# Routed experts of a decoder: one region of rows per expert, routing in five groups of batches, 23 pairs of tiles for 24

## The reference, cut to what matters

```python
logits = x @ gate_w.T                      # 2048 x 8
top, which = top_k(logits, 2)
weight = softmax(top)
y = sum over k of weight[k] * (silu(x @ gate[which[k]].T) * (x @ up[which[k]].T)) @ down[which[k]].T
out = layernorm(x + y)
```

## Time and profile before

| | us |
|---|---|
| median of 3 runs | 3531.8 |
| the profiled execution | 3559.3 |
| its span | 3557.3 |
| TensorE busy in the span | 3178.6 (89%) |
| VectorE busy | 2074.4 (58%) |
| GpSimd busy | 1446.6 (41%) |
| ScalarE busy | 1284.7 (36%) |

### The profile page before, as it was taken

How to read it: one execution, slowest core, us unless ns; L and a number is a source line. 1 busy time by engine, 2 the same in 40 slices (tenths; PEclk the granted TensorE clock), 3 DMA queues, 4 the chain that set the end, 5 groups by cost and what they waited for, 6 DMA issues and landing times. The chain is left out here.

```text
span 3557.3 us, 59026 instructions
## 1 busy us (share of the span) xinstructions
PE 3178.6 (89%) x21124; PEld 2638.1 (74%) x21124; DVE 2074.4 (58%) x3713; ACT 1284.7 (36%) x3287; POOL 1446.6 (41%) x1473
## 2 busy tenths in 40 slices
PE   7999999999969999799896999699999999459992
PEld 5887878878757777677685777588888888258991
DVE  4666666576636666411164666467666677235556
ACT  2333333333256666211103333244444444124440
POOL 3454344444322443300262222355555556155445
PEclk9999999999979999799998999799999999679996
DMA  4001003021120100449472111410101000166664
GB/s 166 21 17 48 0 27 123 0 65 55 52 68 28 51 26 23 182 147 342 150 166 81 39 38 36 142 36 30 34 23 36 22 12 9 43 219 227 241 222 154
DMA packets 129172, 302.42 MB, mean 85 GB/s; under 512 B 18601, under 2 KB 30633, under 8 KB 126466
## 3 DMA queue, kind: packets, MB, share of 16 engines
q1 hardware_dynamic: 111938, 263.14, 22.1%
q0 software_dynamic: 15360, 36.25, 3.8%
q10 hardware_dynamic: 1728, 1.07, 0.1%
HBM read 236.90 MB, written 77.60 MB: 88 GB/s over the span
## 5 line engine op out<-in xcount | busy, mean ns | idle before, releaser
L377 POOL TENSOR_TENSOR a_sq<-a_tq,a_sinq 128x256 f32<-128x256 f32 x128 | 150.1, 1192 | 359.1 <-DVE a_tq L448 359.1
L377 POOL TENSOR_TENSOR a_sk<-a_tk,a_sink 128x256 f32<-128x256 f32 x128 | 123.8, 987 | 90.0 <-DVE a_tk L448 90.0
L343 ACT COPY a_probT<-bank 128x512 f32<-128x512 f32 x64 | 37.5, 586 | 329.0 <-PE bank L653 329.0
L390 POOL TENSOR_TENSOR e_sk<-e_tk 128x512 f32<-128x512 f32 x64 | 66.6, 1040 | 211.2 <-DVE e_tk L475 211.2
L975 POOL TENSOR_TENSOR d_prob<-d_prob,d_nmax 128x1024 f32<-128x1024 f32 x32 | 63.9, 1998 | 197.4 <-DVE d_nmax L1072 197.4
L330 ACT ACTIVATE a_sm<-a_sm,a_nmax 128x128 f32<-128x128 f32 x256 | 99.8, 391 | 121.9 <-DVE a_nmax L535 121.9
L335 ACT ACTIVATE e_prob<-bank,e_nb,e_rq 128x128 f32<-128x128 f32 x256 | 113.8, 455 | 83.1 <-DVE e_nb L540 83.1
L881 ACT ACTIVATE b_prob<-bank,b_nb 128x128 f32<-128x128 f32 x512 | 139.0, 386 | 10.7 <-DVE b_nb L1077 10.3
L2213 POOL TENSOR_TENSOR n_wu_lo<-n_wu,n_wu_hi 128x1408 fp32r<-128x1408 f32 x24 | 77.3, 3221 | 125.0 <-DVE n_wu_hi L2254 125.0
L470 DVE TENSOR_TENSOR a_kr<-a_kr,a_sk 128x512 f32<-128x512 f32 x64 | 66.5, 1038 | 88.9 <-POOL a_sk L377 88.9
L1074 DVE TENSOR_REDUCE b_nmax<-bank 128x8 f32<-128x1024 f32 x64 | 77.7, 1214 | 64.9 <-PE bank L1213 64.5
(11 more groups left out here) (501 smaller groups left out, 10650.6 us busy)
## 6 DMA issues: line engine op xcount, KB each, us to landing
n_wg<-in_f_wg SPq DMA_DIRECT2D x24, 704.0 KB, 4.4
n_wu<-in_f_wu SPq DMA_DIRECT2D x24, 704.0 KB
cw_wg<-in_c_wg SPq DMA_DIRECT2D x32, 512.0 KB
cw_wu<-in_c_wu SPq DMA_DIRECT2D x32, 512.0 KB
cw_wd<-in_c_wd SPq DMA_DIRECT2D x32, 512.0 KB
packed<-all_zero SPq DMA_DIRECT2D x32, 384.0 KB, 4.2
n_xe<-packed SPq DMA_DIRECT2D x48, 256.0 KB
n_wd<-in_f_wd SPq DMA_DIRECT2D x24, 512.0 KB
```

Of the source, the lines that this page charges most:

```text
L343: nc.scalar.copy(probT[:], pP[:, :]).then_inc(act_pt, 1)
L377: step = nc.gpsimd.tensor_tensor(o, i, s, ALU.mult)
```

## The change

The stages `logits_only`, `route` and `dispatch` become one, `spread_routing`. The 16 batches are cut into five groups of 2, 2, 4, 4 and 4. For each batch TensorE makes four transposes and four products with the turned batch as the loaded side, and the router's 8 columns as the moving one, so that the logits come out with tokens in the partitions. VectorE selects group g, then places group g - 1 (for which TensorE has counted), and GpSimd sends a group as soon as it is placed.

For that, the row of a token must not hang on the counts of other experts: `packed2` gets a fixed region of 2048 rows for each expert (16384 rows in all, where it had 6144). After the last group VectorE works out the pairs' experts, the tile at which each pair's rows begin in its region, and the rows in the packed result, which stays as it was. SyncE waits for these tables and loads the weights of the first two pairs in this stage; the weights' buffers and semaphores move to `RoutedWeights`, a stage around both. In `routed_experts` SyncE reads a tile number beside the expert number for each pair. The number of pairs is no longer rounded up to an even one: 23 for 24, 46 tiles for 48, and `in_turns` writes a rest of two tiles out behind the last whole round. Zeroing covers the regions: 128 partitions x 4 rows x 2 KB = 1024 KB for each of the 32 transfers.

```diff
-def in_turns(engine, slot, rounds, ring):
+def in_turns(engine, slot, rounds, ring, rest=0):
     slot(0, 0, back=False)
     with engine.Fori(0, rounds - 1) as i:
@@ -1363,7 +1363,9 @@
             slot(i, n)
         slot(i + 1, 0)
     for n in range(1, ring):
-        slot(rounds - 1, n, ahead=n < ring - 1)
+        slot(rounds - 1, n, ahead=n < ring - 1 or rest > 0)
+    for n in range(rest):
+        slot(rounds, n, ahead=n < rest - 1)
...
+def spread_routing(nc, name, psum, tri, ones, ident, xall, w_dram, packed, NE, weight, rows, weights, NP):
...
+    K, PAIR = 2, 2 * P
+    GROUPS = ((0, 2), (2, 2), (4, 4), (8, 4), (12, 4))
...
+            sp.dma_start(rw[:], w_dram["rw"]).then_inc(c_in, 16)
             sp.dma_start(iota[:], w_dram["iota"]).then_inc(c_in, 16)
+            sp.wait_ge(tabled, 2)
+            for w in range(2):
+                weights.load(sp, weights.number(sp, 0, w), w)
+        def _(pool):
+            for g, (b0, size) in enumerate(GROUPS):
+                pool.wait_ge(v_p, g + 1)
+                for b in range(b0, b0 + size):
+                    for k in range(K):
+                        nc.gpsimd.indirect_dma_start(packed, bass.IndirectOffsetOnAxis(ap=target[:, b, k:k + 1], axis=0), xall[:, b, :],
+                                                     None, bounds_check=NE * REGION - 1, oob_is_err=False).then_inc(sent, 16)
+            pool.wait_ge(sent, 16 * K * B)
...
+            def select(g):
+                b0, size = GROUPS[g]
+                own = slice(b0, b0 + size)
+                dve.wait_ge(pe_l, done(b0 + size - 1))
+                vec.tensor_copy(logits[:, own].rearrange("p b e -> p (b e)"), pL[g % 2][:, 0:NE * size]).then_inc(v_l, 1)
+                dve.wait_ge(v_l, g + 1)
+                for b in range(b0, b0 + size):
+                    last = vec.max(top[:, b], logits[:, b])
                 step(last)
+                for b in range(b0, b0 + size):
+                    last = vec.max_index(topi[:, b], top[:, b], logits[:, b])
                 step(last)
+                step(vec.tensor_copy(topf[:, own], topi[:, own]))
+                each = [P, K, size, NE]
+                step(vec.tensor_tensor(hot[:, :, own], iota[:, 0:NE].unsqueeze(1).unsqueeze(1).to_broadcast(each),
+                                       topf[:, own, 0:K].rearrange("p b k -> p k b").unsqueeze(3).to_broadcast(each), ALU.is_equal))
+                vec.tensor_tensor(sel[:, own], hot[:, 0, own], hot[:, 1, own], ALU.add).then_inc(v_sel, 1)
+            def place(g):
+                b0, size = GROUPS[g]
+                own = slice(b0, b0 + size)
+                dve.wait_ge(pe_c, g + 1)
+                for n in range(size):
+                    step(vec.tensor_tensor(carry[:, b0 + n + 1], carry[:, b0 + n], pC[g % 2][:, P + NE * n:P + NE * n + NE], ALU.add))
+                step(vec.tensor_tensor(pos[:, own], pC[g % 2][:, 0:NE * size].rearrange("p (b e) -> p b e", b=size), carry[:, own], ALU.add))
+                step(vec.tensor_tensor(prod[:, :, own], hot[:, :, own], pos[:, own].unsqueeze(1).to_broadcast([P, K, size, NE]), ALU.mult))
+                step(vec.tensor_reduce(rowf[:, own].rearrange("p b k -> p k b"), prod[:, :, own], AX.X, ALU.add))
+                vec.tensor_copy(target[:, own], rowf[:, own]).then_inc(v_p, 1)
+            for g in range(len(GROUPS)):
+                select(g)
+                if g:
+                    place(g - 1)
+            vec.tensor_tensor(apart[:], top[:, :, 1], top[:, :, 0], ALU.subtract).then_inc(v_c, 1)
+            place(len(GROUPS) - 1)
...
+            vec.tensor_scalar(weights.expert[:], texp[:], float(NE - 1), None, ALU.min).then_inc(tabled, 1)
...
+            vec.tensor_scalar(weights.tile[:], tsum[:], 2.0, float(NE * REGION // P - 2), ALU.mult, ALU.min).then_inc(tabled, 1)
...
+            def turn_x(b):
+                pe.wait_ge(act_x, done(b - 2))
+                for c in range(C):
+                    last = nc.tensor.transpose(pX[b % 2][:, P * c:P * c + P], xall[:, b, P * c:P * c + P], ident[:])
+                last.then_inc(pe_x, 1)
+
+            def logit(b):
+                g = group_of[b]
+                n = b - GROUPS[g][0]
+                pe.wait_ge(act_x, done(b))
+                if g >= 2 and n == 0:
+                    pe.wait_ge(v_l, g - 1)
+                for c in range(C):
+                    last = nc.tensor.matmul(pL[g % 2][:, NE * n:NE * n + NE], xT[:, b % 2, c, :], rw[:, c, :], start=c == 0, stop=c == C - 1)
+                last.then_inc(pe_l, 1)
+
+            def count(g):
+                b0, size = GROUPS[g]
+                pe.wait_ge(v_sel, g + 1)
+                if g >= 2:
+                    pe.wait_ge(v_p, g - 1)
+                own = sel[:, b0:b0 + size].rearrange("p b e -> p (b e)")
+                nc.tensor.matmul(pC[g % 2][:, 0:NE * size], tri[:], own, start=True, stop=True)
+                nc.tensor.matmul(pC[g % 2][:, P:P + NE * size], ones[:], own, start=True, stop=True).then_inc(pe_c, 1)
+
+            turn_x(0)
+            pe.wait_ge(c_in, 32)
             for b in range(B):
+                if b + 1 < B:
+                    turn_x(b + 1)
+                logit(b)
+                g = group_of[b]
+                if g and b == GROUPS[g][0] + 1:
+                    count(g - 1)
+            count(len(GROUPS) - 1)
...
+class RoutedWeights:
...
+    def load(self, sp, e, w):
+        sp.dma_start(self.raw["g"][:, w], self.w_dram["wg"][e]).then_inc(self.gate_in[w], 16)
+        sp.dma_start(self.raw["u"][:, w], self.w_dram["wu"][e]).then_inc(self.up_in[w], 16)
+        for part, name in zip(self.each_down(self.raw["d"], w), ("wd01", "wd2")):
+            sp.dma_start(part, self.w_dram[name][e]).then_inc(self.d_in[w], 16)
...
+    ROUNDS, REST = NT // R, NT % R
+    LAST = (ROUNDS, REST - 1) if REST else (ROUNDS - 1, R - 1)
...
+            def refill(i, w):
+                e, t = weights.number(sp, i + 1, w), place(i + 1, w)
+                sp.wait_ge(pe_x, done(R * i + 2 * w + 1))
+                load_x(t, w)
+                sp.wait_ge(v_gate, done(2 * i + w))
+                sp.wait_ge(g_u, done(2 * i + w))
+                sp.wait_ge(g_d, done(2 * i + w))
+                weights.load(sp, e, w)
+                for n in (2 * w, 2 * w + 1):
+                    store(i, n)
+
+            for w in range(2):
+                load_x(place(0, w), w)
+            with sp.Fori(0, ROUNDS - 1) as i:
                 for w in range(2):
-                    for n in (2 * w, 2 * w + 1):
-                        sp.wait_ge(pe_x, done(R * i + n))
-                        load_x(i + 1, n)
-                    sp.wait_ge(v_gate, done(2 * i + w))
-                    sp.wait_ge(g_u, done(2 * i + w))
-                    sp.wait_ge(g_d, done(2 * i + w))
-                    load(i + 1, w)
-                    for n in (2 * w, 2 * w + 1):
-                        store(i, n)
+                    refill(i, w)
+            for w in range(REST // 2):
+                refill(ROUNDS - 1, w)
+            for n in range(REST, R):
+                store(ROUNDS - 1, n)
+            for n in range(REST):
+                store(ROUNDS, n)
             for n in range(R):
-                store(NT // R - 1, n)
-            for n in range(R):
-                sp.wait_ge(y_out[n], landed(NT // R))
+                sp.wait_ge(y_out[n], landed(ROUNDS + (n < REST)))
...
-NP2 += NP2 % 2
+REGION = B * P
...
-    packed2, result2 = scratch("packed2", NP2 * 2 * P), scratch("result2", NP2 * 2 * P)
+    packed2, result2 = scratch("packed2", 8 * REGION), scratch("result2", NP2 * 2 * P)
...
-            logits_only(nc, "r", psum, ident, xall, w, logits, 8)
-            route(nc, "fr", psum, tri, ones, logits, w, 8, 2, weight, rows, {"pairs": NP2, "expert": expert}, False)
-            dispatch(nc, "fd", xall, rows, packed2, 2, NP2 * 2 * P - 1, [])
-            routed_experts(nc, psum, ident, packed2.rearrange("(t r) d -> t r d", r=P), result2, expert, w, NP2)
+            with ExitStack() as routed:
+                weights = RoutedWeights(Stage(nc, routed, "nw"), w, expert, tile)
+                spread_routing(nc, "r", psum, tri, ones, ident, xall, w, packed2, 8, weight, rows, weights, NP2)
+                routed_experts(nc, psum, ident, packed2.rearrange("(t r) d -> t r d", r=P), result2, weights, NP2)
```

More of the change, by code:

```diff
@@ L1779, in _ @@
+        @block.scalar
+        def _(act):
+            head_start(act, act_x)
+            for b in range(B):
+                act.wait_ge(pe_x, done(b))
+                act.wait_ge(pe_l, done(b - 2))
+                nc.scalar.copy(xT[:, b % 2], pX[b % 2][:, :].rearrange("p (c t) -> p c t", c=C)).then_inc(act_x, 1)
+            act.wait_ge(v_c, 1)
+            nc.scalar.activation(expd[:], apart[:], ACT.Exp).then_inc(act_e, 1)
         @block.vector
         def _(dve):
+            vec = nc.vector
@@ L1781, in _ @@
             step = Chain(dve, v)
[L1782 to L1797 removed]
```

(21 more changed lines are left out.)

328 lines of the change are left out of this document (65 added, 263 removed).

## The result

The changed kernel takes 3511.4 us in the median (3504.3 to 3515.5, 4 runs) against 3532.6 for the kernel before; ratio 0.9934, 95% interval 0.9921 to 0.9946: 21.3 us faster (23 by the ratio). Forecast were 49.5, with 3475 to 3494 as the range. The sign is right, the size is not.

What follows compares the result with a forecast made beforehand. Ahead of the TensorE-bound experts, logits, a VectorE chain and GpSimd's sends were taken to run one after another. 35.1 + 2.2 - 0.5 + 13.7 - 1.0 - 0 = 49.5 us gained gave 3482.3 us, range 3475 to 3494.

Steps and rivals of the forecast that it cites:

- Part 1: Routing: sends run beside counting and logits, so the experts' first transfer comes 35.1 us earlier.
- rival A: Routing: TensorE stays at 1.2 GHz through the logits, as the stream pauses for copies; 5.4 us more, 3487.7; chance 0.13.
- Rival C: End of routing: loads and sends share transfer engines, last rows land after the 4.3 MB; 11.7 us, 3494.0; chance 0.06.
- Part 2: Experts' start: weights of the first two pairs loaded ahead, 2.2 us gained, 0.5 us charged for loads beside sends.
- Part 3: Routed experts: 23 pairs for 24 at 6.86 us a tile, 13.7 us gained.
- Part 4: Before combining: one more barrier closes the weights' stage, costing 1.0 us; SyncE's later reload wait costs nothing.
- Part 5: First attention: zeroing 21 MB more stays hidden, 0 us likeliest, 1.9 us if the burst has a price.
- rival D: First attention: zeroing is not hidden, most of 71 us of extra transfer stands in TensorE's way; 3553; chance 0.03.
- Rival B: Routing: every send beside VectorE is as slow as the slowest was; 7.7 us more, 3490.0; chance 0.06.

Runs made afterwards that it cites:

- filler: The changed kernel with one 512-column float32 product per batch, which nobody reads, added to the routing stage; ratio 0.9929 to the kernel before.
- order: The changed kernel with each group placed on VectorE before the next one is selected, not after; ratio 0.9931 to the kernel before.
- wide2: The changed kernel with router weights stationary for grouped logits, groups placed once selected, and counting of groups 2 and 3 before the next logits; ratio 0.9909.
- one_ahead: The changed kernel with only the first pair's weights loaded ahead, the second pair's following the rows of both; ratio 0.9924 to the kernel before.
- pairs24: The changed kernel with 24 pairs of tiles again instead of 23; ratio 0.9973 to the kernel before.
- reads: The changed kernel with SyncE's two register reads of the next pair put ahead of its waits for the stores; ratio 0.9908 to the kernel before.
- zero2: The changed kernel with a further buffer of 33.5 MB zeroed in the first attention; ratio 0.9931 to the kernel before.
- wide: The changed kernel with router weights stationary for the logits, in the same five groups, each group placed before the next is selected; ratio 0.9939.
- again: The changed kernel run once more, unedited, as a measure beside the others; ratio 0.9932 to the kernel before.
- reads_one: The changed kernel with register reads ahead of the store waits and only the first pair's weights loaded ahead, routing unchanged; 3523.7 us, ratio 0.9918.
- changed: The changed kernel itself, with no further edit; 3511.4 us, ratio 0.9934 to the kernel before.

## Why the prediction was right or wrong

- **Part 1, a batch at the low clock, 1.8 us: wrong, 2.45.** The step that failed is that eight products of the first router "took 1.92, 0.96 for four". A float32 product is two records in the profile: the x8 were one batch's four products, not two batches'. The code, with four products per batch (L1526), said so. By their starts, four transposes now take 0.88 us, as forecast, and a batch's four products 1.57, for 0.96.
- **Part 1, "I let the high clock begin at 3054": wrong.** The clock stayed at 0.50 to the stage's end, which is rival A (0.13). It was priced with the wrong batch: 5.4 us, where the sends end 15.5 us late. 'filler' shows what the clock went with: one wide product per batch, and it rises. How the 15.5 us divide is not shown in full: 'order' takes 4.5 of them away at the low clock, and 'wide2' brings the end to 55.3 us with clock, order and counting changed together. Rival A's reason ("the new stream pauses for its copies") was wrong too; there were no pauses.
- **Part 1, the close of 5.5 us: wrong, 11.3.** Rival C had the mechanism and 0.06; its price, 11.7 us, was for all 4.3 MB after the last send, and 5.8 came. 'one_ahead' takes 4.9 of them away. The argument against it, that most of the loads would be over before the last send, does not agree with Part 2's own sum, by which they run until 3107 beside a last send at 3098.9. At its 166 GB/s some 1.3 MB are left then, 3.6 us at 371 GB/s (an estimate from its numbers); 0.5 us were charged for it, to the rows, and nothing to the close. Measured are 6 us of full transfers after the last send.
- **Part 2: right in sum.** 27.7 us became 24.3, 26.0 were forecast (2.2 gained, 0.5 for contention). The contention was not there: the loads were over 5 us before the first rows' load. What they cost stood in the close.
- **Part 3: right for the pair, wrong for the pace.** The pair is worth 13.8 us, within some 6 ('pairs24'). 9.0 were lost because a tile took 7.06 us, and the step that failed is Part 4's "the slots are needed four tiles (27 us) later, so nothing": I weighed the wait that moved, not the two register reads that now stand ahead of the rows' and the weights' loads, on a queue with little to spare: before, ScalarE used a pair's gate weights 6.6 us after their load was issued (3233.28 to 3239.88), and the load took 4.1 to 5.8 us to land. 'reads' gives all of it back.
- **Part 4, the further close: 0.4 us for 1.0. Part 5 and rival D: zeroing is hidden**, also with 33.5 MB more ('zero2').
- **Rival B: not seen.** The sends beside VectorE's work took 971, 972 and 1115 ns, as those that ran alone did. The case of the Trainium skill (SBUF — State Buffer, section "SBUF: two separate sides"), sends held up by certain VectorE copies between SBUF tiles, does not show among these steps. VectorE's own steps, though, were slow beside the sends in some executions (below).

The range missed because A and C were taken as exclusive cases at small chances, each with its own end; both happened, and with them a third loss that was no rival. The sign held because 49.5 us were forecast and 28.1 lost.

## What to carry to other kernels

When a queue's order changes, count what now stands between the last wait and the loads behind it: 2.2 us of register reads cost 9 us in 23 pairs, because the loads had some 2 us of slack, and putting the reads ahead of the waiting stores gave it back for nothing. Loads put beside sends are in the way of the sends' landing when a barrier waits for it; load only what the first work needs. And check a row's count against the code before dividing it: here a float32 product is two records.

## What the runs showed of the hardware

- TensorE ran without a gap for 35 us at a granted clock of 0.50, in a stream of 128x128 transposes and 8-column float32 products. With one 512-column product per batch more, the clock was 1.00 from 10 us after the stage's start. The Trainium skill (TensorE: Matmul & The Clock Gate, section "HAM oscillation — how this bites in real kernels") lays the low clock to idle gaps between products; here there was none.
- VectorE beside the sends. The same routing code ran its eight chained additions, 0.16 us each, in 1.4 us in one execution (3073.4 to 3074.8) and in 4.9 in another ('reads'):

```profile
3100.62 0.16 DVE L1837 TENSOR_TENSOR r_first<-r_first,r_npair 128x1 f32<-128x1 f32 x1 [1.24 <-DVE r_first L1837]
3101.32 0.35 DVE L1837 TENSOR_TENSOR r_first<-r_first,r_npair 128x1 f32<-128x1 f32 x2 [0.55 <-DVE r_first L1837]
3102.74 0.16 DVE L1837 TENSOR_TENSOR r_first<-r_first,r_npair 128x1 f32<-128x1 f32 x1 [1.07 <-DVE r_first L1837]
```

  Steps then start 0.7 or 1.4 us apart while the sends keep their 1.28. It was seen in 'reads', 'pairs24', 'wide' and, weaker, in 'again' (4.1 us) and 'reads_one' (3.6), and not in the others; with it the weights' loads came 6 to 13 us later than in the changed kernel's first profile. It belongs to the execution, not to an edit: 'again' and 'changed' are one kernel. What causes it stays open. The steps at 3101.32 and 3102.74 began while a send was under way (3100.68 to 3101.65, 3101.96 to 3102.93), so they did not simply wait for its end.
